# Attention with the values' projection behind the q/k projection

## The reference

```python
h = gelu(x[:, 1:] @ W1 + x[:, :1] @ W2 + b)          # 16 batches of 256 rows, 256 wide
z = layernorm(h)
q, k, v = z @ Wq.T, z @ Wk.T, z @ Wv.T               # 16 heads of 64
attn = softmax(q @ k.T * 64 ** -0.5)                 # 255 keys for each row
h = h + (attn @ v) @ Wo.T + bo
z = layernorm(h)
h = h + moe(z)                                       # router, best 2 of 8 experts, a shared expert
```

## Time and profile before

| what | value |
|---|---|
| median of 3 runs | 1192.36 us (1192.11 to 1195.31) |
| the profiled execution | 1195.21 us, span 1193.4 us |
| TensorE busy (PE) | 1070.7 us, 90% of the span |
| VectorE busy | 814.0 us, 68% |
| ScalarE busy | 691.3 us, 58% |
| GpSimd busy | 389.8 us, 33% |

### The profile page before, as it was taken

The page is one execution under the profiler, slowest core; times in us unless marked ns, Lnnn a source line. Parts: engine busy times, 40 slices in busy tenths (PEclk is TensorE's granted clock), DMA queues, the critical chain, the costliest instruction groups (busy, mean ns, idle before and its releaser), DMA issues. The chain is left out here.

```text
span 1193.4 us, 26027 instructions
## 1 busy us (share of the span) xinstructions
PE 1070.7 (90%) x8010; PEld 881.0 (74%) x8011; DVE 814.0 (68%) x2254; ACT 691.3 (58%) x2156; POOL 389.8 (33%) x452
## 2 busy tenths in 40 slices
PE   7979899999999999999999999999976079999897
PEld 6857677768777776777777687777755079999786
DVE  3757767784886688588767858866772456666466
ACT  4647656773775576377647647765761055555454
POOL 0021212242224223322412332241232258745455
PEclk9989999999999999999999999999998589999999
DMA  7110000000001000000000000000001275444564
GB/s 247 54 41 1 1 2 18 2 20 19 18 0 36 18 0 9 27 18 0 36 18 0 9 27 18 0 36 19 2 14 40 73 244 166 134 136 129 193 229 141
DMA packets 46596, 65.56 MB, mean 55 GB/s; under 512 B 7992, under 2 KB 39608, under 8 KB 45496
## 3 DMA queue, kind: packets, MB, share of 16 engines
q1 hardware_dynamic: 36472, 41.48, 11.2%
q0 software_dynamic: 6528, 17.97, 4.2%
q10 hardware_dynamic: 3520, 5.25, 1.4%
HBM read 36.22 MB, written 28.46 MB: 54 GB/s over the span
## 5 line engine op out<-in xcount | busy, mean ns | idle before, releaser
L723 ACT ACTIVATE prob<-s_ps,nmax 128x255 f32<-128x255 f32 x512 | 240.1, 482 | 275.0 <-DVE nmax L836 273.3
L1111 POOL TENSOR_SCALAR prob<-prob,rinv 128x255 f32<-128x255 f32 x128 | 126.6, 989 | 584.9 <-DVE rinv L855 584.9
L836 DVE TENSOR_REDUCE nmax<-s_ps 128x2 f32<-128x510 f32 x256 | 164.8, 674 | 19.0 <-issue 9.4
L581 PE MATMUL o_ps<-probT,v 128*64 128x256 f32 x1024 | 139.8, 392 | 41.6 <-ACT probT L748 39.9
L581 PEld LDWEIGHTS o_ps<-probT,v 128*64 128x64 f32 x1024 | 69.8, 136 | 104.1 <-ACT v L744 58.9
L568 PE MATMUL pT_ps<-ident,prob 128*128 128x128 f32 x1024 | 135.4, 276 | 0.9 <-DVE prob L858 0.9
L568 PEld LDWEIGHTS pT_ps<-ident,prob 128*128 128x128 f32 x1024 | 117.0, 142 | 2.9 <-DVE prob L858 1.8
L858 DVE TENSOR_SCALAR prob<-prob,rinv 128x255 f32<-128x255 f32 x256 | 107.0, 460 | 4.6
L723 ACT ACTIVATION_READ_ACCUMULATOR prob<-s_ps,nmax 128x1 f32 x512 | 108.8, 213 | 0.0
L864 DVE COPY probT<-pT_ps 128x512 f32<-128x512 f32 x128 | 87.0, 680 | 14.9 <-PE pT_ps L568 14.2
L67 PE MATMUL v_ps<-wv_hi,zT_lo 128*128 128x256 f32 x256 | 86.6, 338 | 0.9 <-ACT v L744 0.9
(11 more groups left out here) (253 smaller groups left out, 3007.2 us busy)
## 6 DMA issues: line engine op xcount, KB each, us to landing
xg<-expert_in_rows SPq DMA_DIRECT2D x72, 130.0 KB, 2.2
up_space<-expert_out_rows SPq DMA_DIRECT2D x8, 1024.0 KB, 5.0
xin<-in_x_dram SPq DMA_DIRECT2D x8, 512.0 KB, 4.6
z_rows<-z SPq DMA_DIRECT2D x8, 512.0 KB, 3.2
z<-z_rows ACTq DMA_DIRECT2D x7, 512.0 KB, 3.5
out_dram<-resid SPq DMA_DIRECT2D x8, 256.0 KB, 3.4
out_dram<-resid SPq DMA_DIRECT2D x8, 224.0 KB, 3.3
expert_in_rows<-bo_row SPq DMA_DIRECT2D x12, 128.0 KB
```

The source lines that it names most:

```text
L581: m = pe.matmul(o_ps[h * DH:(h + 1) * DH, 0:N], vt[:, 2 * b + kt, col:col + DH], probT[u_par(i)][:, h, kt, :], start=kt == 0, stop=kt == 1)
L723: m = act.activation(prob[u_par(i)][:, h, qt, 1:N], s_ps[h][:, qt * N + 1:(qt + 1) * N], ACT.Exp, bias=nmax[u_par(i)][:, n:n + 1], accum_o ...
L836: dve.tensor_reduce(nmax[u_par(i)][:, 2 * h:2 * h + 2], s_ps[h][:].rearrange("p (q k) -> p q k", q=2)[:, :, 1:N], AX_X, ALU.max, negate=Tr ...
L1111: pool.tensor_scalar(prob[k][:, 1, 0, 1:N], prob[k][:, 1, 0, 1:N], rinv[k][:, 2:3], None, ALU.mult).then_inc(s_nB, 1)
```

## The change

On TensorE `project_v` leaves its place ahead of the transposes and goes behind the q/k projection, in front of the values. In lap 12, where it already stood behind the transposes, the wait for the next group's `z` moves with the order, to the q/k projection that is now first. On ScalarE `v_copy` leaves its place ahead of `probT_a` and goes behind `qk_hi`. Nothing is added or removed, and no other engine's program changes.

```diff
@@ TensorE @@
                         pe.wait_ge(s_qkl, UNITS * g + ahead - 1)
+                        if i == UNITS - 4:
+                            pe.wait_ge(s_zl, DC * (g + 2))
                         project_qk(g + ahead // UNITS, ahead % UNITS)
 
                     def next_v():
                         if ahead < UNITS or not last:
                             pe.wait_ge(s_ve, UNITS * g + ahead)
-                            if i == UNITS - 4:
-                                pe.wait_ge(s_zl, DC * (g + 2))
                             project_v(g + ahead // UNITS, ahead % UNITS)
 
-                    if i != UNITS - 4:
-                        next_v()
                     transpose_p(g, i)
-                    if i == UNITS - 4:
-                        next_v()
                     next_qk()
+                    next_v()
                     values(g, i)
@@ ScalarE @@
                         exps(*nxt, 0)
-                    if has_tile and i != UNITS - 4:
-                        v_copy(*tile)
                     probT_a(g, i)
-                    if has_tile and i == UNITS - 4:
-                        v_copy(*tile)
                     if has_next:
                         exps(*nxt, 1)
                     if has_tile:
                         qk_hi(*tile)
+                        v_copy(*tile)
                     if has_next:
                         normalise_b1(*nxt)
```

## The result

The changed kernel takes 1178.09 us (median of 4 runs, 1177.01 to 1180.05); the kernel before takes 1192.82 in the same comparison (1192.11 to 1195.31). The ratio is 0.9875, with a 95% interval of 0.9855 to 0.9894. It is faster by 14.7 us, and the prediction of 1178 was right.

The account below looks back on a forecast made before the run. Prediction: a closed cycle of ScalarE and VectorE paces laps without router work, TensorE the router laps. -23 + 11.4 - 2.4 = -14 from 1192.36 gives 1178 us; forecast 1173 to 1184 (0.55), whole range 1164 to 1188.

Parts of the forecast that it names:

- The ring: ScalarE and VectorE's closed cycle sets laps without router work; moving v_copy out cuts 5.53 to 5.26 us: -23 in all.
- The 4 us that I added for laps at a group's start: At group starts and behind router laps, some 20 laps run at TensorE's own pace, gaining 0.2 us more each.
- The router's bank: In laps 4, 5 and 7 the earlier q/k projection waits for VectorE's read: 0.82, 0.66, 0.15 us, +11.4 in all.
- TensorE's new order elsewhere: Same matmuls, and earlier transposes just fit GpSimd's normalisation: taken as 0, with +0.1 us a lap as other bound.
- The clock: At starts of groups 2 to 5, two of four stretches at 1.2 GHz go: -2.4 us, bounds 0 and -4.8.
- The full gain: Rival: router reads cost nothing because VectorE reaches its first maximum earlier; -25, giving 1167 us; chance 0.15.
- The delay by the copy: Rival: v_copy ahead of o_hi delays VectorE's o_lo, so 70 laps lose 9 us: 1187 us; chance 0.12.
- The slower case: Rival: TensorE stands in front of the transposes in every lap, +8 at 0.3 us each: 1200 us; chance 0.07.
- nothing changes: Rival: the stand before the values only moves to the q/k projection, cancelling the gain: 1192 us; chance 0.11.

Follow-up runs that it names:

- ScalarE's order alone: Kernel before with only v_copy moved behind qk_hi on ScalarE, TensorE's order unchanged: 1171.79 us, ratio 0.9817.
- VectorE's loop written out: Kernel before with VectorE's program loop over groups 1 to 5 written out one behind the other: 1184.76 us, ratio 0.9928.
- the pair with the loop written out: VectorE's loop over groups 1 to 5 written out: changed kernel, 1164.96 us; same with TensorE's old order in laps 4, 5, 7, 11, 1156.10 us.
- the router laps back: Changed kernel with the values' projection ahead of the transposes again on TensorE in laps 4, 5, 7 and 11: 1168.61 us, ratio 0.9788.
- the copy at the end: Changed kernel with v_copy moved on behind normalise_b1 and o_hi: 1177.07 us, ratio 0.9857.
- the ring loaded again: Changed kernel with an unread 128x256 ScalarE copy ahead of probT_a in laps 0 to 2 and 8 to 15: 1201.22 us, ratio 1.0056.
- TensorE's order alone: Changed kernel with ScalarE's old order, v_copy ahead of probT_a again: 1327.06 us in one run.

## Why the prediction was right, step by step

*The ring.* Its mechanism stands as predicted: 5.26 us a lap, `probT_a` 0.27 earlier, reproduced by ScalarE's order alone and taken back by the added copy. Its size was about right: the predicted -23 is measured as 1193.24 to 1171.79, -21.5, and the interval of the ratio makes it -19.8 to -23.9. The traces agree. From the first to the last values matmul it is 814.5 us before and 790.5 with ScalarE's order alone; that is 24.1 less. Stretches at the low clock in the trace of before are worth at most 4.4 of it: four of 1.0 at most, and in group 0, which takes 102.4 with VectorE's loop written out and no such stretch in it, against 102.7, one of 0.3. With the estimate of 0.7 for each of the four it is 3.1. That leaves -19.7 to -21.0. The 4 us that I added for laps at a group's start come in groups 1 and 6 (lap 2: 5.55 to 5.09), but not behind a loop's end, where lap 1 now runs at 5.26.

*The router's bank.* Right in kind, in every lap: 4, 5 and 7 lose, 11 gives back in 12. The term was too large: +9.0 us (1177.58 - 1168.61, and 8.9 in the pair with the loop written out) against +11.4. By lap it is 0.70, 0.59 and 0.06 where I had 0.82, 0.66 and 0.15. In lap 4 the stand itself is as predicted, the projection is 0.81 late; the lap is only 0.70 longer because q/k and values' projection together take 0.11 less in the new order: 720.10 - 717.81 = 2.29 from the projection to the values, against 1.58 + 0.82 = 2.40 with the router laps back.

*TensorE's new order elsewhere.* Predicted at nothing, measured at -3.2 (1171.79 to 1168.61), and -3.3 by the traces (groups 1 to 7). This is the step that failed, in the favourable direction. I looked only for waits that it could add, and not for those that it takes away. VectorE's stand for the transposes in lap 8 is gone, and lap 9 gains 0.2 to 0.4 in each of 7 groups, 2.3 us together. That is read from the traces, no run tests it by itself. The laps that TensorE sets are 0.04 shorter, which makes up most of the rest. In lap 8 of group 6 the new order takes 0.85 from the transposes to the q/k projection (0.79 in the old), 1.48 from there to what follows it (1.57), and 0.80 for the values' projection (0.82). Why the same matmuls run shorter in this order no run here tells. The wait for the transposes is there in 51 laps, but small: in the laps of the ring they start 0.98 behind the scores' first matmul instead of 0.91. It ends with VectorE's scaling of head 0 (`prob` L852); the prediction had looked at GpSimd's part alone.

*The clock.* In the profiled pair the four stretches at 1.2 GHz at the starts of groups 2 to 5 are gone: the changed kernel has 1.00 from 69.7 to 875.3 us. But that is one execution of each. Over all executions the mean granted clock is 0.968 for both kernels, and the profiled one of before had 0.965. The traces say the same: from the first to the last values matmul they give 814.5 - 795.2 = 19.3 us less, and without the 4.4 at most for the clock 14.9 or more, where the medians give 14.7. So I count the term of -2.4 as not borne out. The three measured terms cannot decide it: -21.5 + 9.0 - 3.2 = -15.7 are differences along a chain from before to the changed kernel, so they add up to what lies between the two (1193.24 to 1177.58) whatever the clock did. That the stretches made the profiled execution of before some 2 us longer than the median would fit, and is only argued.

*The total.* That the sum hit 1178 is in part luck. The clock's 2.4 that did not come and the 3.2 that were left out nearly cancel, and so do the ring, 1.5 less than predicted, and the bank, 2.4 less.

*The rivals.* The full gain is what the version with the router laps back gives, 1168.61; it would have needed no reads to wait for. The delay by the copy is excluded by the copy at the end and by the 0.38 left ahead of `o_lo`. The slower case needed a stand of 0.25 at the transposes (14 / 112 + 0.1 = 0.23 by its own terms); it is 0.07. That nothing changes fell with the interval of the ratio, and with the ring loaded again, which costs 22 us (ratios 0.987 and 1.0056).

## What to carry to other kernels

When the fullest engine waits a little in every lap, look for the closed ring of two other engines that sets the lap, and move what does not belong in it to a place where its engine is idle: one copy with a price of 0.27 us was worth 21 us here. An order change on the fullest engine is worth testing lap by lap: the same move gained 3 us in one kind of lap and lost 9 in the other, and taking it only where it gains beat both kernels. A stand at a loop's end can cost more than its own length, since the ring starts late behind it: 3.2 us in the changed kernel for a stand of 1.8 on TensorE.

## What was not expected

VectorE's loop stands 2.3 us at its end without issuing; in all, the four times cost 8.5 us in the kernel before and 12.6 in the changed one. For a group with such an end it is 2.1 before (105.80 us from 397.86 to 503.66, less 102.67 with the loop written out, less 1.0 at most for the clock) or a little more, and 3.18 now: the changed kernel's laps 1 to 3 can run at TensorE's own pace, and behind the stand they don't. Why laps 12 and 13 too are 0.7 longer in the loop's form is open.

Where TensorE's clock falls differs from kernel to kernel in ways that I can't explain: at the starts of groups 2 to 5 in the traces of before and of TensorE's order alone, and nowhere from 90 to 840 us in the other traces, although in most of them, the changed kernel's among them, TensorE stands ahead of these groups just the same.
